# Two routings of a four-layer kernel: the operands of the rank products go from fp32 to bf16

## The chip, the cores and the metric

The kernel runs on one core of a Trainium2 chip. The metric is the device time of one execution in microseconds (us). It was timed three times; a fourth execution was recorded by the hardware profiler, and all rows of the trace come from that one.

## What is computed

The input is a batch of 4 x 1024 tokens with 128 features. Four layers follow each other, each added to its input: an attention with 16 heads (causal, rotary), a mixture of experts that sends each token to one of 8 experts, a second attention that looks at 38 fixed offsets, and a second mixture of experts that sends each token to two of 8. Cut to what matters here, the first mixture is

```
logits = x @ router_w + router_b
max_ind = jnp.argmax(softmax(logits), axis=1)
for e in range(8):
    a, g = jnp.split(x @ w1[e], 2, axis=1)
    y = silu(a) * g @ w2[e]
    out = jnp.where((max_ind == e)[:, None], y, out)
out = out * max_prob
```

and the second chooses with `top_k(logits, 2)` and adds the two experts' results with the weights of a softmax. The reference computes every expert for every token. The kernel computes only the chosen ones, and so has to sort the tokens by expert first.

## The kernel before

**The sort.** Both routings work on half a batch at a time: 4 tiles of 128 tokens, 8 halves for each routing. For a half, VectorE writes for each token and expert a 1 where the expert was chosen and a 0 elsewhere: 128 partitions (tokens) by 4 tiles by 8 experts, 32 columns. This is `r.oh`. TensorE then makes the *rank products* (`rk` in the first routing, lines 246 to 254; `rank` in the second, lines 1244 to 1253). One matmul with a strict upper triangle as weights (`tri`, 128 x 128) counts, for each token, the tokens of its tile ahead of it that chose the same expert. Three matmuls with weights of ones (`one`) add to each tile the counts of the tiles before it, and four more with the ones sum the half into 8 columns. These are 8 matmuls, each with its own load of 128 x 128 weights. VectorE adds the running `base` of each expert, picks the chosen expert's position (`rpos` at lines 299 to 309, `pos` at lines 1327 to 1337), and GpSimd scatters the token's row to that position in memory with an indirect DMA (`send0`, `send`).

**The stages.** The program has four stages with a barrier between them, and each engine walks through one written-out list of work items in each stage; each engine executes its own part of it in order.

- Attention 0 (0 to 860 us of the trace). 32 units of two heads. TensorE makes scores twice: once for the row maxima (line 561, taken by VectorE at lines 775 and 778), once for the probabilities (line 572, exponentiated by ScalarE at line 666), then the product with V (line 589). SyncE copies the rotated Q and K for four units at a time (line 495). The halves of the first three batches are routed beside it, at the steps of the table `ROUTES`. All products share a ring of three PSUM tiles S.
- Expert layer 0 (860 to 1100 us). It begins with the two halves of the last batch, interleaved with a small chain of 128 x 128 products for a matrix exponential (lines 998 and 1128). Only when the last half is ranked does VectorE know where each expert's rows end (`tiles0`), and only then can SyncE fetch the sorted rows.
- Attention 1 (1100 to 1411 us). 32 tiles of 128 tokens, with the second routing for five of its halves beside it (table `STEPS1`). TensorE makes scores at line 1540, VectorE takes them at line 1701, probabilities are transposed (line 1557) and multiplied with V (line 1566).
- Expert layer 1 (1411 to 1667 us). It begins with the other three halves of the second routing. Beside them TensorE makes the dense products `ab` (lines 1944 and 1945). When the eighth half is ranked, the sorted rows are fetched and the experts run.

**The choices' path in the second routing.** `top` (VectorE) writes `r.o0` and `r.o1`, the first and the second choice, and their sum `r.oh` (tile `ohs`, line 1326); `rank` (TensorE) waits for it; `pos` (VectorE) waits for `rank` and is queued ahead of `q3` of the next half on VectorE, whose result `n2` TensorE transposes (`nT`) before it makes the next logits (`lg1`).

**What a wait is.** `dve.then(ins)` makes VectorE wait for its own instruction `ins` before it goes on, since a read behind a write on one engine is not ordered otherwise.

I number the rank products by time: r1 to r8 for the first routing (at 367, 473, 565, 671, 764, 841, 881 and 890 us), q1 to q8 for the second (at 1245, 1288, 1333, 1374, 1402, 1453, 1469 and 1485 us).

Of the kernel before, what the change touches and what calls it, by code (L numbers as in the profile page):

```python
# [6 lines left out]
F32 = mybir.dt.float32  # L7
F32R = mybir.dt.float32r
BF16 = mybir.dt.bfloat16
U32 = mybir.dt.uint32  # L10
ALU = mybir.AluOpType
# [77 lines left out]
class Program:  # L89
# [41 lines left out]
    def sb(self, st, name, shape, dt=F32):  # L131
        return st.enter_context(self.nc.sbuf_tensor(name, shape, dt))
# [55 lines left out]
class Route0:  # L188
    loads = ("rw", "iota", "rb", "tri", "one", "base", "first", "idn")

    def __init__(self, p, st):
        def sb(name, shape, dt=F32):
            return p.sb(st, name, shape, dt)

        self.xs = p.nc.dram_tensor("xs", (8 * CAP + 128, RW0), F32, kind="Internal").ap()
        self.small = {n: sb(n + "0", [128, w]) for n, w in
                      (("rw", 8), ("iota", 8), ("rb", 8), ("tri", 128), ("one", 128), ("base", 8), ("first", 8), ("idn", NT))}
        self.lg, self.m8, self.d8, self.ex, self.oh, self.pa = (sb(n, [128, 4, 8]) for n in ("lg0", "m80", "d80", "ex0", "oh0", "pa0"))
        self.i8, self.fi, self.sm, self.posf = sb("i80", [128, 4, 8], U32), sb("fi0", [128, 4]), sb("sm0", [128, 4]), sb("posf0", [128, 4])
        self.posu, self.share = [sb(f"posu0{q}", [128, 4], U32) for q in range(3)], sb("share", [128, 32])  # L200
        self.xr, self.xT = [], []
        self.n, self.slot = {}, {}
# [32 lines left out]
def route0_tensor(p, r, pe, te, w):  # L235
    s, S, m, q = w.slot, p.S, r.small, room0(w)
    if w.kind == "rT":
        pe.wait_ge(p.sem("v_xr"), w.n)
        turn_over(te, p, S[s], r.xr[q][:, :, 0:128], 4).then_inc(p.made("rT").h, 1)
    elif w.kind == "rl":  # L240
        pe.wait_ge(p.sem("d_r0"), 16 * len(r.loads))
        pe.wait_ge(p.done("rT"), w.n)
        for i in range(4):
            ins = te.matmul(S[s][:, 8 * i:8 * i + 8], r.xT[q][:, 128 * i:128 * i + 128], m["rw"][:], start=True, stop=True)
        ins.then_inc(p.made("rl").h, 1)
    elif w.kind == "rk":
        pe.wait_ge(p.sem("v_hot"), w.n)
        oh = r.oh[:].rearrange("p n e -> p (n e)")
        te.matmul(S[s][:, 0:32], m["tri"][:], oh, start=True, stop=False)
        for d in range(1, 4):  # L250
            te.matmul(S[s][:, 8 * d:32], m["one"][:], oh[:, 0:32 - 8 * d], start=False, stop=(d == 3))
        for i in range(4):
            ins = te.matmul(S[s][:, 64:72], m["one"][:], oh[:, 8 * i:8 * i + 8], start=(i == 0), stop=(i == 3))
        ins.then_inc(p.made("rk").h, 1)


# [13 lines left out]
def route0_vector(p, r, dve, ve, w):  # L270
    S, s, m, q = p.S, w.slot, r.small, room0(w)
    n = 8 * w.at[0] + 4 * w.at[1]
    if w.kind == "rn":
        dve.wait_ge(p.sem("v_mean"), r.n[w.at])
        dve.wait_ge(p.sem("g_rstd"), r.n[w.at])
        dve.wait_ge(p.sem("d_r0"), 16 * len(r.loads))
        if not q:
            dve.wait_ge(p.sem("v_spin"), min(8 * B, 4 * (2 * w.at[0] + w.at[1] + 4)))
            if w.n > 1:
                dve.wait_ge(p.sem("d_sc0"), 64 * (w.n - 1))  # L280
        ve.tensor_copy(r.xr[q][:, :, 128:RW0], m["idn"][:, n:n + 4, None].broadcast_to([128, 4, RW0 - 128]))
        ln_apply(p, ve, r.xr[q][:, :, 0:128], p.x[:, n:n + 4, :], range(4)).then_inc(p.sem("v_xr").h, 1)
    elif w.kind == "rl":
        dve.wait_ge(p.made("rl"), w.n)
        ve.tensor_tensor(r.lg[:], S[s][:, 0:32].rearrange("p (n e) -> p n e", e=8),
                         m["rb"][:, None, :].broadcast_to([128, 4, 8]), ALU.add).then_inc(p.done("rl").h, 1)
        dve.wait_ge(p.done("rl"), w.n)
        for i in range(4):
            ins = ve.max(r.m8[:, i, :], r.lg[:, i, :])
        dve.then(ins)  # L290
        ve.tensor_tensor(r.d8[:], r.lg[:], r.m8[:, :, 0:1].broadcast_to([128, 4, 8]), ALU.subtract).then_inc(p.sem("v_negmax").h, 1)
        for i in range(4):
            ins = ve.max_index(r.i8[:, i, :], r.m8[:, i, :], r.lg[:, i, :])
        dve.then(ins)
    elif w.kind == "rhot":
        dve.then(ve.tensor_copy(r.fi[:], r.i8[:, :, 0]))
        ve.tensor_tensor(r.oh[:], m["iota"][:, None, :].broadcast_to([128, 4, 8]), r.fi[:, :, None].broadcast_to([128, 4, 8]),
                         ALU.is_equal).then_inc(p.sem("v_hot").h, 1)
    elif w.kind == "rpos":
        s = r.slot["rk", w.at[0], w.at[1]]  # L300
        dve.wait_ge(p.made("rk"), w.n)
        dve.then(ve.tensor_tensor(r.pa[:], S[s][:, 0:32].rearrange("p (n e) -> p n e", e=8), m["base"][:, None, :].broadcast_to([128, 4, 8]), ALU.add))
        ve.tensor_tensor(m["base"][:], m["base"][:], S[s][:, 64:72], ALU.add).then_inc(p.done("rk").h, 1)
        dve.then(ve.tensor_tensor(r.pa[:], r.pa[:], r.oh[:], ALU.mult))
        dve.then(ve.tensor_reduce(r.posf[:], r.pa[:], AX.X, ALU.add))
        ve.tensor_copy(r.posu[q][:], r.posf[:]).then_inc(p.sem("v_pos0").h, 1)
        dve.wait_ge(p.sem("a_ex"), w.n)
        dve.then(ve.tensor_reduce(r.sm[:], r.ex[:], AX.X, ALU.add))
        dve.then(ve.reciprocal(r.share[:, n:n + 4], r.sm[:]))
# [191 lines left out]
def attn0_tensor(p, k, pe, te):  # L501
    S, A, W = p.S, p.A, k.W
    for w in k.items:
# [3 lines left out]
        if w.kind in ("rT", "rl", "rk"):  # L507
            route0_tensor(p, k.route, pe, te, w)
# [687 lines left out]
RW, G, NC1, NQ1 = 144, 4, 8, 3  # L1196


class Route1:
    loads = ("mw", "mb", "base", "first", "idt", "cols")  # L1200

    def __init__(self, p, st, first):
        def sb(name, shape, dt=F32):
            return p.sb(st, name, shape, dt)

        def two(name, shape, dt=F32):
            return [sb(f"{name}{i}", shape, dt) for i in range(2)]

        self.xq = p.nc.dram_tensor("xq", (8 * CAP + 128, RW), F32, kind="Internal").ap()
        self.small = {n: sb(n + "1", [128, w]) for n, w in (("mw", 8), ("mb", 8), ("base", 8), ("first", 8), ("cols", 3))}  # L1210
        self.small["idt"] = sb("idt", [128, 32, 2])
        self.small.update({n: first.small[n] for n in ("iota", "tri", "one")})
        self.n1, self.nT = two("n1", [128, G, 128]), sb("nT", [128, NC1, 128 * G])
        self.n2 = [two(f"n2{q}", [128, G, RW]) for q in range(NQ1)]
        self.stats, self.mv, self.rs = sb("stats1", [128, G, 6]), sb("mv1", [128, G, 2]), sb("rs1", [128, G])
        self.lg, self.m8 = sb("lg1", [128, G, 8]), sb("m81", [128, G, 8])
        self.i8, self.fi = sb("i81", [128, G, 8], U32), sb("fi1", [128, G, 2])
        self.dd = sb("dd", [128, NT])
        self.o0, self.o1, self.oh = (sb(n, [128, G, 8]) for n in ("o0", "o1", "ohs"))
        self.pa, self.m0, self.m1 = (sb(n, [128, G, 8]) for n in ("pa", "m0", "m1"))  # L1220
        self.posf, self.posu = sb("posf", [128, 2, G]), [sb(f"posu{q}", [128, 2, G], U32) for q in range(NQ1)]
        self.bank, self.placed = {}, set()
# [10 lines left out]
def route1_tensor(p, r, pe, te, w):  # L1233
    m, c = r.small, w.at[0]
    if w.kind == "nT":
        pe.wait_ge(p.sem("v_n2"), c + 1)
        turn_over(te, p, r.bank["nT", c], r.n2[c % NQ1][0][:, :, 0:128], G).then_inc(p.made("nT").h, 1)
    elif w.kind == "lg1":
        bank = r.bank["lg1", c]
        pe.wait_ge(p.done("nT"), c + 1)  # L1240
        for i in range(G):
            ins = te.matmul(bank[:, 8 * i:8 * i + 8], r.nT[:, c, 128 * i:128 * i + 128], m["mw"][:], start=True, stop=True)
        ins.then_inc(p.made("lg1").h, 1)
    elif w.kind == "rank":
        bank = r.bank["rank", c]
        pe.wait_ge(p.sem("v_oh"), c + 1)
        oh = r.oh[:].rearrange("p n e -> p (n e)")
        te.matmul(bank[:, 0:8 * G], m["tri"][:], oh, start=True, stop=False)
        for d in range(1, G):
            te.matmul(bank[:, 8 * d:8 * G], m["one"][:], oh[:, 0:8 * (G - d)], start=False, stop=(d == G - 1))  # L1250
        for i in range(G):
            ins = te.matmul(bank[:, 64:72], m["one"][:], oh[:, 8 * i:8 * i + 8], start=(i == 0), stop=(i == G - 1))
        ins.then_inc(p.made("rank").h, 1)


# [1073 lines left out]
```

## Time and profile before

| | us |
|---|---|
| median of three timed executions | 1683.62 |
| lowest and highest of them | 1682.8 and 1690.06 |
| the profiled execution, its own time | 1668.86 |
| span of the trace, first to last instruction | 1667.1 |

The profiled execution is 14.8 us shorter than the median, so a sum in its microseconds is carried over as a difference, not as a time. Its busiest engine is TensorE (82% of the span), then VectorE (69%). The granted TensorE clock is 0.874 of full speed on average; it is always at one of two levels, 2.4 GHz (1.0) or 1.2 GHz (0.5), and the mean says how the time is shared between them.

In the rows, PE is TensorE's matmuls, PEld its weight loads, DVE VectorE, ACT ScalarE, POOL GpSimd and SPq the queue in which SyncE issues transfers. L253 is line 253 of the kernel.

### The profile page before, as it was taken

To read this page: it belongs to the slowest core of one execution; us is meant where nothing else is said; L and a number is where in the kernel's file an instruction comes from. 1 tells how busy PE (TensorE), PEld (TensorE's weight loads), DVE (VectorE), ACT (ScalarE), POOL (GpSimd) and SP (SyncE) were. 2 spreads that over 40 slices of the span, in tenths; PEclk is the share of its full clock that TensorE was granted. 3 is DMA by queue.
4 is the path that set the end of the run, shared out by engine and by line. 5 is a ranking of instruction groups with operands and counts; after the bars stand their busy time and mean duration, and the time that the engine had idled before them with its cause. 6 is when DMAs were issued, how large, how long until landed. Compare 5 with 4: busy or idle time off the path is not lost.

```text
span 1667.1 us, 37536 instructions
## 1 busy us (share of the span) xinstructions
PE 1368.6 (82%) x13404; PEld 903.3 (54%) x13404; DVE 1153.7 (69%) x3796; ACT 723.6 (43%) x1523; POOL 697.4 (42%) x1004
## 2 busy tenths in 40 slices
PE   4479889998998889989967999498898997886771
PEld 2244444454454544545446666377777776665660
DVE  4568697887979878888834544369999977144445
ACT  1135455555555545555630334155544431115553
POOL 3013232232423323342221223478878885264554
PEclk9679999999999999999975999778978776558995
DMA  4654717455373735737224011121111111212324
GB/s 101 93 95 75 116 25 113 76 89 88 46 125 53 118 56 71 125 45 124 32 98 154 24 31 40 31 71 50 41 41 47 49 49 37 77 54 72 83 79 159
DMA packets 73724, 123.13 MB, mean 74 GB/s; under 512 B 17505, under 2 KB 45928, under 8 KB 72645
## 3 DMA queue, kind: packets, MB, share of 16 engines
q1 hardware_dynamic: 64820, 106.67, 33.9%
q0 software_dynamic: 7616, 13.59, 2.5%
q8 instruction: 109, 1.79, 0.5%
q10 hardware_dynamic: 1104, 0.48, 0.1%
q14 instruction: 75, 0.61, 0.1%
HBM read 30.34 MB, written 17.60 MB: 29 GB/s over the span
## 4 chain that ended last, share of the span: by engine, by line
PE 47%; DVE 23%; SPq 11%; issue 7%; DMA 4%; ACT 4%; POOL 2%; ACTq 0%; POOLq 0%; DVEq 0%
SPq L495 9%; DVE first L775 5%; PE A L589 4%; PE S L1029 4%; PE S L572 3%; PE S L1540 3%; DVE S L778 3%; PE S L561 3%; PE A L1973 3%; PE S L1966 2%; PE A L1551 2%; DVE tA L754 2%; PE S L553 2%; PE A L1041 2%; DVE tB L755 2%
## 5 line engine op out<-in xcount | busy, mean ns | idle before, releaser
L666 ACT ACTIVATE P<-S 128x512 f32<-128x512 f32 (+3 forms) x768 | 332.2, 490 | 290.5 <-PE S L572 285.0
L561 PE MATMUL S<-Kp,Qp 120*128 120x512 f32 (+3 forms) x768 | 254.6, 401 | 43.7 <-issue 15.6
L849 POOL TENSOR_SCALAR_AFFINE_SELECT P<-P 128x256 f32<-128x256 f32 (+1 forms) x256 | 117.4, 462 | 401.5 <-ACT P L666 400.5
L572 PE MATMUL S<-Qp,Kp 121*128 121x512 f32 (+3 forms) x768 | 252.8, 393 | 32.6 <-DVE tB L755 9.2
L778 DVE CUSTOM_DVE_ANT_0 S<-S,later 128x512 f32<-128x512 f32 (+3 forms) x512 | 239.4, 514 | 50.8 <-PE S L561 43.6
L561 PEld LDWEIGHTS S<-Kp,Qp 120*128 120x128 f32 x768 | 134.5, 197 | 178.7 <-issue 80.5
L775 DVE TENSOR_REDUCE first<-S 128x1 f32<-128x512 f32 x256 | 164.5, 684 | 52.4 <-PE S L561 52.3
L572 PEld LDWEIGHTS S<-Qp,Kp 121*128 121x128 f32 x768 | 140.1, 193 | 108.9 <-issue 24.9
L589 PE MATMUL A<-P,V 128*9 128x512 f32 (+3 forms) x1536 | 176.6, 508 | 4.6 <-POOL P L849 4.2
L2104 POOL DMA_INDIRECT yq<-yq,id x71 | 69.5, 978 | 66.1 <-DVE yq L2068 35.1
L1773 POOL TENSOR_TENSOR prod<-qf,kT 128x128 f32<-128x128 f32 x160 | 73.1, 490 | 38.8 <-ACT qf L1608 20.1
L1188 POOL DMA_INDIRECT ys<-yo,id x39 | 38.2, 980 | 107.9 <-DVE yo L1168 104.0
L1540 PE MATMUL S<-kT,Qm 32*32 32x64 f32 x4096 | 64.9, 235 | 22.4 <-issue 11.9
L1352 POOL DMA_INDIRECT xq<-n,posu x64 | 68.7, 1073 | 30.1 <-DVE posu L1336 15.7
L1029 PE MATMUL S<-w,xgT 128*128 x156 | 76.8, 616 | 3.8 <-issue 2.4
L1159 DVE SCALAR_TENSOR_TENSOR uu<-th,S 128x512 f32<-128x512 f32 x39 | 26.9, 689 | 68.5 <-ACT th L1061 58.1
L778 DVE DVE_READ_ACCUMULATOR2_ANT mx<- 128x1 f32 x512 | 72.2, 141 | 0.0
L1540 PEld LDWEIGHTS S<-kT,Qm 32*32 32x32 f32 x4096 | 49.6, 110 | 39.0 <-issue 21.4
L1656 ACT ACTIVATE pt<-S 128x1024 f32<-128x1024 f32 x32 | 32.7, 1023 | 64.7 <-PE S L1557 63.5
L1973 PE MATMUL A<-er,hq 128*128 x284 | 51.2, 304 | 8.2 <-issue 3.7
L1966 PE MATMUL S<-xqT,wq 128*128 128x128 f32 x284 | 48.6, 296 | 10.7 <-ACT xqT L2002 9.9
L754 DVE TENSOR_TENSOR tA<-S,cos 128x512 f32<-128x512 f32 x60 | 41.2, 686 | 21.7 <-PE S L553 12.0
(333 smaller groups left out, 2793.5 us busy)
## 6 DMA issues: line engine op xcount, KB each, us to landing
Qp<-rcq SPq DMA_DIRECT2D x64, 256.0 KB
Kp<-rck SPq DMA_DIRECT2D x64, 256.0 KB
Qp<-rcq SPq DMA_DIRECT2D x64, 128.0 KB
Kp<-rck SPq DMA_DIRECT2D x64, 128.0 KB
xq<-xq SPq DMA_DIRECT2D x71, 72.0 KB
yb<-yq SPq DMA_DIRECT2D x8, 528.0 KB, 4.4
Qp<-cq SPq DMA_DIRECT2D x64, 64.0 KB
Kp<-ck SPq DMA_DIRECT2D x64, 64.0 KB
```

The lines of the kernel that those rows point to most:

```text
L495: ye.dma_start(rows, src).then_inc(p.sem(f"d_q{u % 4}").h, 16)
L561: te.matmul(S[s][:, 512 * h:512 * h + n], Q[0:120, h, 128 * qt:128 * qt + 128], K[0:120, h, 512 * part:512 * part + n], start=True, stop=T ...
L572: te.matmul(S[s][:, 512 * h + c:512 * h + 512], K[0:121, h, 128 * kb:128 * kb + 128], Q[0:121, h, 512 * qh + c:512 * qh + 512], start=True ...
L589: ins = te.matmul(A[oa][o:o + 9, c:512], k.V[u // 8 % 2][:, kb, 2 * (u % 8) + h, :], k.P[(e.n - 1) % NP0][:, h, c:512], start=kb < 2, stop ...
L666: se.activation(k.P[(w.n - 1) % NP0][:, h, c:512], S[s][:, 512 * h + c:512 * h + 512], ACT.Exp, scale=SCALE0).then_inc(p.done("st").h, 1)
L775: ve.tensor_reduce(k.first[:, h, qt - 4:qt - 3], S[s][:, 512 * h:512 * h + 512], AX.X, ALU.max).then_inc(p.done("mx").h, 1)
L778: ins = ve.tensor_tensor_reduce(out=of, in0=of, in1=k.later[:, 512 - n:512], scale=1.0, scalar=-3e38, op0=ALU.add, op1=ALU.max, accum_out= ...
L849: ge.affine_select(P[:, :, start:c + 128], P[:, :, start:c + 128], [[0, 2], [1, wide]], ALU.is_ge, 0.0, base=start - c, channel_multiplier ...
L1029: ins = te.matmul(S[s][:, c:c + 512], k.xgT[t % NH][:], k.w1[:, bass.ds(expert[t] * 1024 + c, 512)], start=True, stop=True)
L1540: ins = te.matmul(C[32 * q:32 * q + 32, 64 * h:64 * h + 64], k.Qm[c % 2][rows, j, 128 * i + 32 * q:128 * i + 32 * q + 32], k.kT[c % 2][row ...
L1966: ins = te.matmul(S[s][:, c], k.w[t % 4][:, c], k.xT[t % 4][:], start=True, stop=True)
L1973: ins = te.matmul(A[s][:, 0:129], k.h[t % 4][:, 128 * j:128 * j + 128], k.er[:, bass.ds(expert * 258 + 129 * j, 129)], start=(j == 0), sto ...
```

## The change

The choices `r.oh`, the triangle and the ones become bf16 tiles where a matmul reads them. All values are 0, 1 or 2 at most, which bf16 holds exactly; the sums in PSUM stay fp32.

- The triangle and the ones are still loaded in fp32, and VectorE copies each once into a bf16 tile (`tri16`, `one16`) at the first `rhot`.
- In the first routing VectorE still writes `r.oh` in fp32, because `rpos` multiplies with it; it now waits for it and copies it into a bf16 tile `hot0`. The signal `v_hot`, for which TensorE waits, moves to that copy.
- In the second routing the sum `ohs` is written as bf16 directly. It is read by the matmuls alone, so no instruction is added there.

No work item moves on any engine. VectorE gains 10 instructions (8 copies of 128 x 32, two of 128 x 128); the other engines keep theirs.

```
-        te.matmul(S[s][:, 0:32], m["tri"][:], oh, start=True, stop=False)
+        te.matmul(S[s][:, 0:32], r.tri[:], r.hot[:], start=True, stop=False)
         for d in range(1, 4):
-            te.matmul(S[s][:, 8 * d:32], m["one"][:], oh[:, 0:32 - 8 * d], start=False, stop=(d == 3))
+            te.matmul(S[s][:, 8 * d:32], r.one[:], r.hot[:, 0:32 - 8 * d], start=False, stop=(d == 3))
         for i in range(4):
-            ins = te.matmul(S[s][:, 64:72], m["one"][:], oh[:, 8 * i:8 * i + 8], start=(i == 0), stop=(i == 3))
+            ins = te.matmul(S[s][:, 64:72], r.one[:], r.hot[:, 8 * i:8 * i + 8], start=(i == 0), stop=(i == 3))
         ins.then_inc(p.made("rk").h, 1)
...
     elif w.kind == "rhot":
         dve.then(ve.tensor_copy(r.fi[:], r.i8[:, :, 0]))
-        ve.tensor_tensor(r.oh[:], m["iota"][:, None, :].broadcast_to([128, 4, 8]), r.fi[:, :, None].broadcast_to([128, 4, 8]),
-                         ALU.is_equal).then_inc(p.sem("v_hot").h, 1)
+        dve.then(ve.tensor_tensor(r.oh[:], m["iota"][:, None, :].broadcast_to([128, 4, 8]), r.fi[:, :, None].broadcast_to([128, 4, 8]), ALU.is_equal))
+        if w.n == 1:
+            ve.tensor_copy(r.tri[:], m["tri"][:])
+            ve.tensor_copy(r.one[:], m["one"][:])
+        ve.tensor_copy(r.hot[:], r.oh[:].rearrange("p n e -> p (n e)")).then_inc(p.sem("v_hot").h, 1)
...
-        self.o0, self.o1, self.oh = (sb(n, [128, G, 8]) for n in ("o0", "o1", "ohs"))
+        self.o0, self.o1, self.oh = (sb(n, [128, G, 8], dt) for n, dt in (("o0", F32), ("o1", F32), ("ohs", BF16)))
...
-        te.matmul(bank[:, 0:8 * G], m["tri"][:], oh, start=True, stop=False)
+        te.matmul(bank[:, 0:8 * G], r.tri[:], oh, start=True, stop=False)
         for d in range(1, G):
-            te.matmul(bank[:, 8 * d:8 * G], m["one"][:], oh[:, 0:8 * (G - d)], start=False, stop=(d == G - 1))
+            te.matmul(bank[:, 8 * d:8 * G], r.one[:], oh[:, 0:8 * (G - d)], start=False, stop=(d == G - 1))
         for i in range(G):
-            ins = te.matmul(bank[:, 64:72], m["one"][:], oh[:, 8 * i:8 * i + 8], start=(i == 0), stop=(i == G - 1))
+            ins = te.matmul(bank[:, 64:72], r.one[:], oh[:, 8 * i:8 * i + 8], start=(i == 0), stop=(i == G - 1))
```

## Rows read from the trace of the kernel before

**Rows 1.** Windows; busy PE, PEld, DVE, ACT, POOL; granted clock, DMA share, GB/s

```profile
1180.00:1415.00 235.00, 204.55 (x5104) 171.79 (x5093) 209.99 (x565) 93.39 (x139) 184.06 (x251) 0.77 0.16 45
1415.00:1508.00 93.00, 72.01 (x262) 56.55 (x262) 28.11 (x164) 13.65 (x21) 35.36 (x39) 0.54 0.20 67
```

**Rows 2.** Line 1330's answer: what it waited for, us in total, times

```profile
  PE A L1252: 18.8, 3
```

**Rows 3.** Chain that ended last, at r1: start us, us, what

```profile
367.61 0.14 PE S L249 x2
367.75 0.65 PE S L251 x6
368.40 0.89 PE S L253 x8
```

**Rows 4.** The same chain at r8

```profile
890.72 0.27 PE S L249 x2
890.98 1.24 PE S L251 x6
892.22 1.71 PE S L253 x8
```

**Rows 5.** The same chain at q7

```profile
1469.08 0.56 PE A L1248 x2
1469.64 1.24 PE A L1250 x6
1470.88 1.72 PE A L1252 x8
```

**Rows 6.** The same chain behind q1, products with V

```profile
1247.32 0.67 PE A L1566 x50
```

**Rows 7.** The same chain between r1 and r3, beside r2

```profile
470.96 1.97 SPq L495
```

**Rows 8.** Timeline, VectorE in attention 0: start, us, line; idle before it, releaser

```profile
369.33 0.19 DVE L302 TENSOR_TENSOR pa<-S,base 128x32 f32<-128x32 f32 x1 [0.47 <-PE S L253]
371.89 1.29 DVE L775 TENSOR_REDUCE first<-S 128x1 f32<-128x512 f32 x2 [0.66 <-PE S L561]
...
570.49 1.29 DVE L775 TENSOR_REDUCE first<-S 128x1 f32<-128x512 f32 x2 [0.94 <-PE S L561]
...
767.87 0.69 DVE L775 TENSOR_REDUCE first<-S 128x1 f32<-128x512 f32 x1 [0.34 <-PE S L561]
...
843.37 0.19 DVE L302 TENSOR_TENSOR pa<-S,base 128x32 f32<-128x32 f32 x1 [1.98 <-PE S L253]
```

**Rows 9.** Timeline, VectorE at the start of expert layer 0

```profile
880.15 0.16 DVE L296 CAST fi<-i 128x4 f32<-128x4 uint32 x1
880.34 0.19 DVE L297 TENSOR_TENSOR oh<-iota,fi 128x32 f32<-128x32 f32 x1
...
883.70 0.19 DVE L302 TENSOR_TENSOR pa<-S,base 128x32 f32<-128x32 f32 x1 [0.73 <-PE S L253]
...
890.75 0.56 DVE L1128 TENSOR_TENSOR F<-S,G 128x384 f32<-128x384 f32 x1 [1.50 <-PE S L998]
...
893.97 0.19 DVE L302 TENSOR_TENSOR pa<-S,base 128x32 f32<-128x32 f32 x1 [2.26 <-PE S L253]
```

**Rows 10.** Timeline, VectorE: a copy of 128 x 128

```profile
1418.37 0.22 DVE L2038 COPY Rg<-R 128x128 f32<-128x128 f32 x1
```

**Rows 11.** Timeline, VectorE behind q2, q3 and q4

```profile
1306.98 1.23 DVE L1701 TENSOR_TENSOR sc<-S,near 128x1024 f32<-128x1024 f32 x1 [0.43 <-PE S L1540]
...
1341.10 1.22 DVE L1701 TENSOR_TENSOR sc<-S,near 128x1024 f32<-128x1024 f32 x1 [2.96 <-PE S L1540]
...
1386.19 0.24 DVE L1704 TENSOR_TENSOR sc<-A,far 128x80 f32<-128x80 f32 x1 [1.02 <-PE A L1551]
```

**Rows 12.** Timeline, GpSimd's indirect DMAs ahead of and behind q8

```profile
1483.58 0.96 POOL L1352 DMA_INDIRECT xq<-n,posu  x1 [0.31 <-issue]
...
1490.37 1.16 POOL L1352 DMA_INDIRECT xq<-n,posu  x1 [5.83 <-DVE posu L1336]
```

More of the change, by code:

```diff
@@ L198, in __init__ @@
         self.lg, self.m8, self.d8, self.ex, self.oh, self.pa = (sb(n, [128, 4, 8]) for n in ("lg0", "m80", "d80", "ex0", "oh0", "pa0"))
+        self.hot = sb("hot0", [128, 32], BF16)
+        self.tri, self.one = sb("tri16", [128, 128], BF16), sb("one16", [128, 128], BF16)
         self.i8, self.fi, self.sm, self.posf = sb("i80", [128, 4, 8], U32), sb("fi0", [128, 4]), sb("sm0", [128, 4]), sb("posf0", [128, 4])
@@ L247, in route0_tensor @@
         pe.wait_ge(p.sem("v_hot"), w.n)
-        oh = r.oh[:].rearrange("p n e -> p (n e)")
-        te.matmul(S[s][:, 0:32], m["tri"][:], oh, start=True, stop=False)
+        te.matmul(S[s][:, 0:32], r.tri[:], r.hot[:], start=True, stop=False)
         for d in range(1, 4):
-            te.matmul(S[s][:, 8 * d:32], m["one"][:], oh[:, 0:32 - 8 * d], start=False, stop=(d == 3))
+            te.matmul(S[s][:, 8 * d:32], r.one[:], r.hot[:, 0:32 - 8 * d], start=False, stop=(d == 3))
         for i in range(4):
-            ins = te.matmul(S[s][:, 64:72], m["one"][:], oh[:, 8 * i:8 * i + 8], start=(i == 0), stop=(i == 3))
+            ins = te.matmul(S[s][:, 64:72], r.one[:], r.hot[:, 8 * i:8 * i + 8], start=(i == 0), stop=(i == 3))
         ins.then_inc(p.made("rk").h, 1)
@@ L1211, in __init__ @@
         self.small["idt"] = sb("idt", [128, 32, 2])
-        self.small.update({n: first.small[n] for n in ("iota", "tri", "one")})
+        self.small["iota"], self.tri, self.one = first.small["iota"], first.tri, first.one
         self.n1, self.nT = two("n1", [128, G, 128]), sb("nT", [128, NC1, 128 * G])
```

## The prediction

> **What bounds the kernel now.** I read the page first. TensorE is busy 82% of the span and VectorE 69%, so a saving of TensorE time can count, but neither number says where. The windows by stage say more [rows 1]: in the middle of attention 1 (235 us) VectorE is busy 210.0 us and TensorE 204.6 us, two engines about equally close to the bound; at the start of expert layer 1 (93 us) TensorE is busy 72.0 us at a granted clock of 0.54, almost all at the lower level, and VectorE only 28.1 us. The time of a rank product is therefore worth something different at each of its 16 places. So I read the chain that ended last at each place, then the waits of VectorE behind it in the timeline.
>
> At full clock a rank product is 16 records, two for each of its 8 matmuls, and takes 0.14 + 0.65 + 0.89 = 1.68 us of the chain, 0.105 us a record [rows 3]. At the lower level it is 0.27 + 1.24 + 1.71 = 3.22 us, 0.201 us a record [rows 4]. The columns (32, 24, 16 or 8) make no difference that one can see, so it is the weights that are paid for. r1 to r7, q1, q2, q3 and q5 ran at the full level, r8, q4, q6, q7 and q8 at the lower one.
>
> **Price of a bf16 matmul.** The trace has no bf16 matmul. The upper bound is one record as it stands, 0.105 us (0.201 at the lower level): half the records, none of them faster. The lower bound is the cheapest record in the trace, line 1566 with 32 columns of weights: 0.67 us for 50, 0.013 us each [rows 6]. Those load a quarter of the columns; four of them would be 0.054 us. Between ends eight times apart I go by that row, scaled to the columns, and take half a record: 0.0525 us, or 0.10 us at the lower level. A product then costs 8 x 0.0525 = 0.42 us instead of 1.68, or 0.80 us instead of 3.22: it saves 1.26 us at full clock and 2.42 us at the lower one. By the bounds it saves 0.84 to 1.57 us, or 1.61 to 3.11 us.
>
> The Trainium skill, page "TensorE: Matmul & The Clock Gate", section "LDWEIGHTS (loading the stationary operand)", speaks against the half record: a load takes as many ns as its columns divided by 1.2, and no type is named there, which for 128 columns is 107 ns. That is close to the trace's record at full clock, and by it the saving would be near my lower bound. The page "FP8 and Floating Point Precision" of the Trainium skill, section "TensorE Precision Notes", has true fp32 as 4 passes through the array, which by itself gives a quarter. No run so far tells them apart.
>
> **Attention 0.** VectorE gains a wait for its own comparison and a small copy in each `rhot`. A conversion and the comparison behind it, with the same kind of wait between them, start 0.19 us apart [rows 9], so I take 0.2 us a place. The two copies of 128 x 128 come once, ahead of r1: 0.22 us for such a copy [rows 10], less where one overlaps the next, so 0.35 us for both. Behind the `rhot`, TensorE is still busy with queued scores for 2 to 3 us, so `v_hot` coming later holds up no matmul; what it costs is VectorE's own time, where VectorE leads to the next scores.
> - r1: VectorE waits 0.47 us for the product and 0.66 us for scores right behind it [rows 8]. These 1.13 us are what it can get back, less 0.2 and 0.35: 0.6 us.
> - r3: 0.47 (as at r1) and 0.94 us [rows 8], more than the 1.26 us saved; less 0.2: 1.1 us.
> - r5: 0.47 and 0.34 us [rows 8], less 0.2: 0.6 us.
> - r2 and r4: nothing. Around r2 the chain is SyncE's issue of one transfer after the other [rows 7], and around r4 too; TensorE ends by waiting for the last of them.
> - r6: VectorE waits 1.98 us for it [rows 8] and ScalarE waits for the scores behind it: all of 1.3 us.
>
> Sum 3.6 us. By the bounds of the price 2.4 us, or 4 x 1.57 = 6.3 us without the copies.
>
> **Expert layer 0.** The copy is hidden: after r8's comparison VectorE waits 1.50 us for TensorE anyway [rows 9]. At r7 VectorE waits 0.73 us for the product, because it has work for line 1131 until then; more it can't get back. At r8 it waits 2.26 us of the 2.42 [rows 9]; the product of line 998 queued behind r8 starts when VectorE's line 1131 lets it, so of these I take 2.0. The ends of the experts' rows, the pads, the fetches of sorted rows and the matrix exponential all follow. Sum 2.7 us; bounds 0.7 + 1.6 = 2.3 and 0.73 + 2.26 = 3.0 us.
>
> **Attention 1.** Nothing is added on VectorE. A shorter product counts only if VectorE next waits for TensorE. Behind q1 it has no such wait before q2, and behind q5 TensorE waits for VectorE: 0. Behind q2 the first wait is 0.43 us, behind q3 2.96 us (so all 1.26), behind q4 1.02 us [rows 11]. Sum 2.7 us. The bounds are 0, if TensorE's lead runs into the next slot of PSUM each time, and 9.4 us, if every product counts whole at the cheapest price (4 x 1.57 + 3.11).
>
> **Expert layer 1.** Here the products stand bare in the chain: q7 is 0.56 + 1.24 + 1.72 us, of which 0.29 is the first record's latency and stays [rows 5]. VectorE waits 18.8 us in three times for q6, q7, q8 and the dense products ahead of them [rows 2], and everything of the next half is queued on VectorE behind `pos`. So 3 x 2.42 = 7.3 us. GpSimd could take the place: its indirect DMAs of the halves before run one behind the other until 1484.5 us, and it then waits 5.83 us for q8's positions [rows 12]. That stream moves ahead with q6 alone (2.42 us), q8's positions with all three (7.3): 4.9 of the 5.83 us are used, and 0.9 stays. It is not late yet. Bounds 3 x 1.61 = 4.8 us, and 5.83 + 3.11 = 8.9 us, where GpSimd becomes the later.
>
> **Sum.** 3.6 + 2.7 + 2.7 + 7.3 = 16.3 us. From the profiled execution's 1668.86 us that gives 1652.6; from the median of 1683.62, which is 14.8 us higher for the same program, 1667.3, rounded to 1667. The bounds are 2.4 + 2.3 + 0 + 4.8 = 9.5 us and 6.3 + 3.0 + 9.4 + 8.9 = 27.6 us, so 1656.0 to 1674.1.
>
> **The rivals.**
> - *A bf16 load is no cheaper than a record.* All products save the lower bound: 9.5 us, 1674. For it: the record's time doesn't depend on the moving columns [rows 3]. This is where the rule on LDWEIGHTS of the Trainium skill, page "TensorE: Matmul & The Clock Gate", would end. Chance 0.12.
> - *VectorE takes it all in the attentions.* Nothing is gained there and the copies are paid in full, 6 x 0.2 + 0.35 = 1.6 us: 2.7 + 7.3 - 1.6 = 8.4 us, 1675. For it: its 210.0 busy us of 235 [rows 1], and that in attention 0 the chain passes through it as much as through TensorE. Against: the waits of rows 8. Chance 0.12.
> - *More comes back.* TensorE is really the bound in attention 1 as well, as the chain there says, which lies on it behind every product: 5 us more there and the cheaper load elsewhere, some 25 us, 1659. Chance 0.12.
> - *Slower: the granted clock.* Attention 1 runs at 0.77 [rows 1], so 46% of it at the lower level. Where TensorE has less to do it has been granted the lower level: 0.54 at the start of expert layer 1, with 72.0 busy us of 93. If shorter products tip more of attention 1 to it, its 204.6 busy us stretch with 0.77 over the new clock. A clock of 0.713 eats the whole 16.3 us; from 0.69 on the kernel is slower by over 0.5%; at 0.68 it is 27 - 16 = 11 us, 1694. Against: q1 to q5 are under 5% of that stage's TensorE work. Chance 0.06.
>
> **Chances and range.** 0.58 for the forecast, whose own range is 1661 to 1673, and the rest as above. A measurement of this kernel tells about 0.5%, 8.4 us, from no change. The forecast and the rival with more end below 1675.2 but for small parts; of the first two rivals, which lie within a microsecond of that line, I count half. That is 0.54 + 0.12 + 0.12 = 0.78 for faster, 0.15 for within 0.5%, 0.07 for slower. The range takes in the bounds of the price and, above, a few of the 7 us by which the three timed executions differ: 1656 to 1679.
>
> **What the next profile would show.** One record for each matmul in place of two (line 1252's group on the ring A: 12, not 24), 0.05 us apart at full clock. VectorE's three waits at the line after `rank` fall from 18.8 to about 11.5 us, and GpSimd's wait ahead of q8's sends to about 1 us. From the start of expert layer 1 to its first expert the time falls by 7 us. Attention 1 shortens by less than its products do, and VectorE's busy time stays. The forecast is wrong if records are 0.1 us apart (price), if the last half's positions come 7 us earlier but its transfers don't (GpSimd or SyncE), or if the clock of attention 1 moves by more than 0.03 either way, which alone is worth 8 us.

## The result, and the profile after

| | median, us | runs, us | ratio to before, 95% interval |
|---|---|---|---|
| before, beside it | 1683.21 | 1678.27 to 1690.06 | |
| the change | 1665.26 | 1651.54 to 1671.35 | 0.9900, 0.9854 to 0.9945 |
| the change in a later job | 1666.07 | 1656.06 to 1672.9 | 0.9918, 0.9882 to 0.9953 |

The change is 14 to 17 us faster. The two profiled executions don't show it: 1668.86 us before, 1668.63 us after. So I read the trace by stage and over all profiles of the study, never by the difference of two spans.

The windows of [rows 1], in the profile of the change:

```profile
1180.00:1415.00 235.00, 200.63 (x4818) 164.81 (x4816) 203.06 (x553) 89.36 (x133) 173.13 (x240) 0.70 0.14 40
1415.00:1508.00 93.00, 68.11 (x242) 51.79 (x243) 28.07 (x164) 14.29 (x22) 35.58 (x39) 0.50 0.19 67
```

TensorE is busy 4 us less in each. The granted clock is lower in both, 0.70 for 0.77 and 0.50 for 0.54. In the first, attention 1, the 4 us hide two larger terms, which are taken apart below.

The chain that ended last, at q7, beside [rows 5]:

```profile
1469.74 0.14 PE A L1252
1469.88 0.07 PE A L1254 x3
1469.95 0.12 PE A L1256 x4
1470.07 0.02 issue
1470.09 0.20 DVE pa L1334
```

One record a matmul in place of two, and the product is 0.14 + 0.07 + 0.12 = 0.33 us at the lower level, where it was 3.52 us. The matmuls stand 0.02 to 0.03 us apart, though a load by itself lasts 0.1 us: they overlap. At full clock (r6) it is the same:

```profile
835.71 0.12 PE S L250
835.83 0.07 PE S L252 x3
835.89 0.10 PE S L254 x4
```

What VectorE waited for at line 1334 (before line 1330, [rows 2]), and then the timeline at q8, GpSimd and SyncE's queue included:

```profile
  remote: 7.4, 1
  PE A L1256: 5.8, 2
```

The three waits are 13.2 us together, where the prediction had about 11.5. At q8:

```profile
1482.86 0.25 PE L1256 MATMUL A<-ohs,one 128*128 128x8 bf16 x4
1483.28 0.95 POOL L1356 DMA_INDIRECT xq<-n,posu  x1 [0.30 <-issue]
1484.54 0.96 POOL L1356 DMA_INDIRECT xq<-n,posu  x1 [0.30 <-issue]
1486.62 0.19 DVE L1334 TENSOR_TENSOR pa<-A,base 128x32 f32<-128x32 f32 x1 [7.37 <-remote]
1488.01 1.16 POOL L1356 DMA_INDIRECT xq<-n,posu  x1 [2.52 <-DVE posu L1340]
1488.77 12.15 SPq L1908 DMA_DIRECT2D xq<-pads  x8
...
1502.93 0.36 SPq L1918 DMA_DIRECT2D xq<-xq  x1
```

Here is something that I had not foreseen. The product's last matmul ends at 1482.86 + 0.25 = 1483.11 us. VectorE waits for that alone and starts 3.5 us later; the trace calls the releaser "remote", which means that it has none. GpSimd's wait, 5.83 us in [rows 12], is 2.52 us. SyncE's eight pads (the rows that fill up each expert's last tile) then take 12.15 us to issue and the first rows are fetched 2.0 us behind the last. At q6 a send (an indirect DMA that GpSimd issues) runs across the product's end too, and VectorE starts 0.03 us behind the product:

```profile
1456.79 0.25 PE L1256 MATMUL A<-ohs,one 128*128 128x8 bf16 x4
1456.99 0.96 POOL L1356 DMA_INDIRECT xq<-n,posu  x1 [0.30 <-issue]
1457.07 0.19 DVE L1334 TENSOR_TENSOR pa<-A,base 128x32 f32<-128x32 f32 x1 [4.30 <-PE A L1256]
```

### The profile page after: what moved, and what is told of

It is laid out like the page before. It is cut to its first block, busy times and chain, and to the rows that moved or that the text cites. A ratio compares the mean times of both kernels' runs of the same rounds, so it can differ in the third digit from the quotient of the medians.

```text
span 1666.7 us, 37290 instructions
## 1 busy us (share of the span) xinstructions
PE 1358.0 (81%) x13276; PEld 888.0 (53%) x13276; DVE 1156.7 (69%) x3806; ACT 723.5 (43%) x1523; POOL 693.7 (42%) x1004
## 4 chain that ended last, share of the span: by engine, by line
PE 43%; DVE 25%; SPq 9%; issue 8%; POOL 5%; DMA 5%; ACT 4%; another core or an unknown queue 1%; ACTq 0%; POOLq 0%; DVEq 0%
SPq L499 8%; DVE first L779 5%; PE S L1033 4%; PE A L593 4%; DVE S L782 3%; PE S L576 3%; PE S L565 3%; PE S L1544 3%; PE A L1977 2%; PE S L1970 2%; PE A L1555 2%; PE A L1045 2%; DVE tA L758 2%; PE S L179 2%; PE S L557 2%
## 5 line engine op out<-in xcount | busy, mean ns | idle before, releaser
L1544 PE MATMUL S<-kT,Qm 32*32 32x64 f32 x4096 | 66.0, 244 | 18.4 <-issue 7.2
```

The costliest lines, as they stand in the source:

```text
L1544: ins = te.matmul(C[32 * q:32 * q + 32, 64 * h:64 * h + 64], k.Qm[c % 2][rows, j, 128 * i + 32 * q:128 * i + 32 * q + 32], k.kT[c % 2][row ...
```

## The experiments

Twelve runs in three jobs, each job with its own runs of the kernel before. Two of them repeat a kernel: the change, and the version without copies.

**1. One routing at a time.** In the first, only the first routing is bf16, with the copies. In the second only the second, without `hot`; the two copies of 128 x 128 stay. A part of the edit of the first, against the change (triangle and ones go back to fp32 as well):

```diff
-        self.o0, self.o1, self.oh = (sb(n, [128, G, 8], dt) for n, dt in (("o0", F32), ("o1", F32), ("ohs", BF16)))
+        self.o0, self.o1, self.oh = (sb(n, [128, G, 8], dt) for n, dt in (("o0", F32), ("o1", F32), ("ohs", F32)))
```

> Only the first routing's rank products (r1 to r8) are bf16, with the copies of the change; the second routing's are fp32 as before. My sum gives it 3.6 us in attention 0 and 2.7 us in expert layer 0: ratio to the kernel before about 0.996. If VectorE takes the gain in attention 0, as the two profiles hint (4.5 of the first 7.4 us by which the changed kernel is ahead at the end of attention 0 are there before r1), only expert layer 0 counts: 1.5 to 2.5 us, ratio 0.999.

> Only the second routing's rank products (q1 to q8) are bf16; the first routing's are fp32 as before, without its small copy (the two copies of the triangle and the ones remain). My sum gives 2.7 us in attention 1 and 7.3 us in expert layer 1: ratio about 0.994. If a bf16 matmul costs 0.03 us, as the changed kernel's profile shows, the three products of expert layer 1 give 8 to 9 us. If the granted clock of attention 1 falls with it (0.70 in the changed kernel's profile, 0.77 before), nothing may be left: ratio 0.998 to 1.0.

Measured: 0.9958 (0.993 to 0.9986) and 0.9968 (0.9936 to 0.9999) of 1680.02 us, 7.0 and 5.4 us. The first routing gives about what I forecast (6.3 us), the second about half (10.0), each with an interval of some 5 us either way. The alternative for the first, a ratio of 0.999, lies outside. The second's profile shows where more is lost at q8:

```profile
1488.60 14.65 SPq L1909 DMA_DIRECT2D xq<-pads  x8
1499.33 1.08 ACT L1993 ACTIVATE ab<-S 128x512 f32<-128x512 f32 x2 [15.24 <-remote]
1505.26 0.36 SPq L1919 DMA_DIRECT2D xq<-xq  x1
```

VectorE's positions are 3 us earlier than in the kernel before, but the pads take 14.65 us to issue, and ScalarE too waits for something that the trace doesn't have. The kernel before, same rows:

```profile
1491.13 10.93 SPq L1904 DMA_DIRECT2D xq<-pads  x8
1504.07 1.49 SPq L1914 DMA_DIRECT2D xq<-xq  x2
```

**2. bf16 without a copy.** Triangle and ones come from memory as bf16, and the comparison writes its 0 and 1 as bf16 itself; the positions are still fp32. The change once more and a repeat of this version follow. The edit against the change, in part:

```diff
-        self.hot = sb("hot0", [128, 32], BF16)
+        self.oh = sb("oh0", [128, 4, 8], BF16)
...
-        dve.then(ve.tensor_tensor(r.oh[:], m["iota"][:, None, :].broadcast_to([128, 4, 8]), r.fi[:, :, None].broadcast_to([128, 4, 8]), ALU.is_equal))
-        if w.n == 1:
-            ve.tensor_copy(r.tri[:], m["tri"][:])
-            ve.tensor_copy(r.one[:], m["one"][:])
-        ve.tensor_copy(r.hot[:], r.oh[:].rearrange("p n e -> p (n e)")).then_inc(p.sem("v_hot").h, 1)
+        ve.tensor_tensor(r.oh[:], m["iota"][:, None, :].broadcast_to([128, 4, 8]), r.fi[:, :, None].broadcast_to([128, 4, 8]),
+                         ALU.is_equal).then_inc(p.sem("v_hot").h, 1)
...
-        "tri": (k[:, None] < k[None, :]).astype(np.float32),
+        "tri": (k[:, None] < k[None, :]).astype(mybir.dt.np(BF16)),
```

> The change without its copies: the triangle and the ones arrive as bf16 from memory, and the first routing writes its choices as bf16 directly and multiplies with them in that type. VectorE loses 10 instructions and 8 waits for itself, 2 us of its own time. If VectorE bounds attention 0, it is 1 to 2 us faster than the change (ratio to before about 0.989); if the copies are hidden, the same as the change.

> The change once more, unaltered, against the kernel before. Both theories have it at 1665 to 1668 us, a ratio of 0.990 to 0.992. What it settles is whether the version with the 0/1 operands written as bf16 at their source (1657.66 us, ratio 0.987, in an earlier job) is really faster than the change: the seven VectorE copies that it drops in the first routing's ramp and row are worth 8 x 0.2 us plus two of 0.22 us at most, so theory 1 (the copies cost what they last) has the two 2 us apart or less, and a gap of 5 us or more here again would mean that something other than the copies' own time is saved. The wait of VectorE's first instruction behind the eighth rank product of the second routing ends again some 3 us after the product does if that stall belongs to the kernel, and at once if it was chance.

> The version with no copy at all, once more, beside the two above: 1653 to 1659 us, ratio 0.985 to 0.988 in each theory. The add behind the eighth product of the second routing starts 2 to 3.5 us late again, since GpSimd's sends run at that moment.

Measured: 1657.66 us, 0.9870 (0.9839 to 0.9902), and in another job 1652.56 us, 0.9846 (0.9796 to 0.9895). The change again is 1666.07 us, 0.9918. The gap of 5 us or more that theory 1 excluded is there again, though in different jobs. Beside the change itself ran a version without copies with 60 idle writes added (part 5): 0.9862 for 0.9918, 9 us, give or take 10. Over all, two measurements with the copies have a mean ratio of 0.9909 and the four without the small ones 0.9861 (the three here and one of part 3): 8 us, give or take 6. So the copies cost more than the 1.6 us that I had given them.

**3. Which copy.** The first has bf16 choices at the source but still copies triangle and ones once; the second is the kernel before, fp32 throughout, with all of the change's copies added, read by nobody. A part of the second's edit against the change:

```diff
-        te.matmul(S[s][:, 0:32], r.tri[:], r.hot[:], start=True, stop=False)
+        oh = r.oh[:].rearrange("p n e -> p (n e)")
+        te.matmul(S[s][:, 0:32], m["tri"][:], oh, start=True, stop=False)
```

> The change with the 0/1 choices of the first routing written as bf16 by the comparison itself, so that the eight copies hot and their waits are gone; triangle and ones are still copied once. Stage times of the profiles so far, attention 0 from the second addition to x to its end: 559 to 562 us in three profiles with copies, 554 to 556 in three without, 562 to 571 with fp32. Theory K (the eight copies, with the add of their own wait and the 0.62 us that one lasts beside GpSimd, cost those 5 us): this one lies with the version without any copy, 1654 to 1659 us, ratio 0.985 to 0.988. Theory L (the two 128x128 copies in the first row cost it, one of them 0.57 us at 358): it lies with the change, 1664 to 1667 us. Theory M (5 us are where chance put those six profiles): all three are alike within 2 us in this job.

> The kernel before, all products in fp32, with only the change's copies and their waits added (their results are read by nobody). Theory K: 4 to 6 us slower than before, ratio 1.0025 to 1.0035. Theory L: the same 4 to 6 us. Theory M: 8 x 0.23 us and the row's 0.4 us at most, under 2 us, ratio 1.000 to 1.001. If copies cost 5 us with fp32 too, their price is VectorE's and not that of the earlier start of anything.

Measured: 1656.23 us, 0.9866 (0.9814 to 0.9918), where the versions without copies lie; and 1683.93 us, 1.0041 (1.0001 to 1.0081), so 7 us slower by the ratio, with an interval from 0.2 to 14 us. The times point to theory K, that it is the eight small copies and their waits, but don't show it: the first kernel alone, set against the change, is 7 us better with an interval of 10 either way, and the second has all ten copies. A part of the cost can be seen. VectorE's copy beside a mask of GpSimd's, in the profile of the change at r3:

```profile
556.07 0.62 POOL L853 TENSOR_SCALAR_AFFINE_SELECT P<-P 128x512 f32<-128x512 f32 x1 [0.47 <-ACT P L670]
556.10 0.62 DVE L302 CAST hot<-oh 128x32 bf16<-128x32 f32 x1
...
664.83 0.18 DVE L302 CAST hot<-oh 128x32 bf16<-128x32 f32 x1
```

It ends when GpSimd's instruction does, 0.62 us instead of 0.18. That happens to one or two of eight, to the copy of the triangle as well (0.57 us); with the starts 0.23 us apart and 0.62 us for the two of the first row the sum is 8 x 0.23 + 2 x 0.44 + 0.62 = 3.3 us at most. The rest I can't place.

**4. Doubled, and six times.** All fp32 rank products of the kernel before issued twice; those of the second routing alone; and in the version without copies the bf16 products of the first routing six times. The edit of the second routing, in part:

```diff
-        te.matmul(bank[:, 0:8 * G], m["tri"][:], oh, start=True, stop=False)
+        for _ in range(2):
+            te.matmul(bank[:, 0:8 * G], m["tri"][:], oh, start=True, stop=False)
```

> The kernel before with every fp32 rank product issued twice (the second overwrites the first with the same sums). TensorE gets 1.68 us more at full clock or 3.22 us more at the lower level at 16 places. If TensorE's time at these places counts as in my sum, the loss is 1.2 to 1.3 times the forecast gain, 20 us, ratio 1.012. If VectorE hides them in the attentions, only the start of the two expert layers counts: 3 x 3.22 + 1.7 + 3.2 = 14.6 us, ratio 1.009. If a longer busy TensorE is granted more of the full clock in attention 1, it is less than that.

> The kernel before with its eight fp32 rank products of the second routing issued twice; the first routing is as before. Both routings doubled cost 45 us, where the products' own time, all of it on the path, is 8 x 1.68 us for the first routing and 5 x 1.68 + 3 x 3.22 us for the second, 31 us in all. If each routing is amplified alike, this one costs 22 to 28 us (1702 to 1708 us); if the extra in both was the first routing's (20 us in attention 0 and 9 us ahead of expert layer 0 in that profile), it costs 10 to 18 us (1690 to 1698 us).

> The version with no copy, with each bf16 product of the first routing issued six times, 48 multiplications in place of 8. Eight more of them take 0.25 to 0.29 us in a row by the records of the change, so five more products add 1.25 to 1.45 us to each of eight places, about what the fp32 form had more than the bf16 form (1.68 less 0.33 us). If TensorE's time in the row is all that counts, this takes back what the first routing won without copies: 8 x 1.35 = 11 us, 1664 to 1668 us. If extra TensorE time in attention 0 is amplified, as doubling fp32 there seemed to say (45 us for both routings less 20 for the second leaves 25 us for 13.4 us of products), it is 18 to 22 us, 1674 to 1678 us.

Measured: 1.0273 (1.0224 to 1.0322), 1.0112 (1.0057 to 1.0167) and 0.9863 (0.9811 to 0.9915). The first is 46 us (38 to 54), more than twice the 20 that I expected. I had scaled the forecast gain, which is capped where VectorE's wait ends, while added time has no such cap: all the products are 33.1 us, at the levels of the clock that they had before. The levels moved too: r7, at full clock before, ran at the lower one in both of its copies. Doubling the second routing costs 19 us by the ratio, what its products are worth with all of them on the path (5 x 1.68 + 3 x 3.22 = 18.1 us). The first routing takes the other 0.016, 27 us, give or take 12, for 7 x 1.68 + 3.22 = 15.0 us of products; whether that is more than they are worth isn't shown. Six bf16 products in a row, at r1:

```profile
364.36 0.19 PE L252 MATMUL S<-oh,tri 128*128 128x32 bf16 x1
364.40 0.22 PE L254 MATMUL S<-oh,one 128*128 128x24 bf16 x3
364.47 0.24 PE L256 MATMUL S<-oh,one 128*128 128x8 bf16 x4
364.57 0.18 PE L252 MATMUL S<-oh,tri 128*128 128x32 bf16 x1
364.60 0.22 PE L254 MATMUL S<-oh,one 128*128 128x24 bf16 x3
364.67 0.24 PE L256 MATMUL S<-oh,one 128*128 128x8 bf16 x4
364.77 0.18 PE L252 MATMUL S<-oh,tri 128*128 128x32 bf16 x1
```

A product takes 0.20 us, 0.025 a matmul. Five more at each of eight places are 8.0 us of TensorE, not the 11 that I expected; the ratio has moved by 0.0017 against the same version with single products in the same job, 3 us, with an interval that takes in 8 and 0 but not the 18 to 22 us of an amplified cost. In its one profile attention 0 is 6.5 us longer than in the five others without the small copies (563.3 for a mean of 556.8), and the products added there are 6 x 1.0 us: what is added is about what is paid.

**5. The late start at q8.** In the version without copies: first 60 short VectorE writes more, hidden in a 7 us wait, which shift its instruction stream; second, four of GpSimd's sends held back until the last positions are there.

```diff
+    for j in range(12):
+        for t in k.yo:
+            ve.memset(t[:, 8 * j:8 * j + 1], 0.0)
```

```diff
-        pool.wait_ge(p.sem("v_pos"), c + 1)
+        pool.wait_ge(p.sem("v_pos"), NC1 if (c, h) == (NC1 - 2, 1) else c + 1)
```

> The version without copies, with 60 short VectorE writes of one column more at the start of expert layer 1, where VectorE waits 7 us for a load and has nothing else to do. It moves every later VectorE instruction 60 places down its instruction stream and costs nothing on the path (60 x 0.07 us = 4 us inside a 7 us wait). Theory S (the late start behind the eighth rank product is the stream being fetched): the late start of 2.0 to 3.5 us moves away from that place or changes to under 0.5 us. Theory G (something of GpSimd's sends, which run at that moment): it stays at 2 us or more. Theory C (chance): it is gone, and e5 and e7 show it or not without pattern. Time as the version without copies, 1655 to 1661 us, in each theory.

> The version without copies, with the last four sends of the seventh group (second half of its rows) held back on GpSimd until the positions of the eighth group are there. GpSimd is then idle when the eighth rank product ends. Theory G: VectorE's add behind that product starts within 0.3 us of the product's end. Theory S: still 2 to 3 us late. In both the sends end later: GpSimd has 12 sends of 1.26 us behind the eighth positions instead of 8, so expert layer 1's first expert starts 5 us later less what the earlier positions give back (2 to 3 us in theory G): about 1660 us.

The stream shifted:

```profile
1467.41 0.25 PE L1254 MATMUL A<-ohs,one 128*128 128x8 bf16 x4
1467.85 0.96 POOL L1354 DMA_INDIRECT xq<-n,posu  x1 [0.30 <-issue]
1469.12 0.96 POOL L1354 DMA_INDIRECT xq<-n,posu  x1 [0.30 <-issue]
1470.41 0.19 DVE L1332 TENSOR_TENSOR pa<-A,base 128x32 f32<-128x32 f32 x1 [6.60 <-remote]
```

The sends held back:

```profile
1468.90 0.25 PE L1254 MATMUL A<-ohs,one 128*128 128x8 bf16 x4
1469.19 0.19 DVE L1332 TENSOR_TENSOR pa<-A,base 128x32 f32<-128x32 f32 x1 [3.88 <-PE A L1254]
...
1470.57 1.16 POOL L1354 DMA_INDIRECT xq<-n,posu  x1 [4.07 <-DVE posu L1338]
```

Shifted, VectorE is 2.75 us late as before. Held back, it starts 0.04 us after the product, and the wait has its releaser again. In the eight profiles with bf16 in the second routing and the sends running it is 2.0 to 3.5 us late each time; in the five with fp32 never, since there the product ends when the sends are through. That speaks for theory G, that the late start needs GpSimd's row of sends, and against theory S; but the held-back case has one profile, and the sends alone don't do it: in the same eight profiles a send is under way or begins within 0.25 us at the end of q6's product, and VectorE starts there within 0.04 us of it. What holds VectorE up, the runs don't say. Holding back wins nothing here, since the sends end later (first fetch 17.7 us behind `endi`; one execution, 1654.05 us); the shifted version is 1653.61 us, 0.9862 (0.9817 to 0.9907), a third measurement without copies.

## The stages, over all profiles

Worked out from the timelines, one profile a kernel: attention 0 from VectorE's second to its eighth addition to x, attention 1 from its first to its eighth, the start of expert layer 0 up to the first fetch of sorted rows, that of expert layer 1 from q6's logits (line 1312 before) to the copy `endi`, and from there to the first fetch. The number of profiles stands in brackets. Doubled products are left out, and the six-fold and held-back kernels where they touch the stage.

| stage, us | fp32 there | bf16 there | gain | forecast |
|---|---|---|---|---|
| attention 0, no copies `hot` | 561.9, 570.7, 565.5 | 555.4, 556.4, 554.1, 558.1, 560.0 | 9.2 | |
| attention 0, with copies | 566.2 | 558.9, 560.9, 561.7 | | 3.6 |
| start of expert layer 0 | 46.1 to 48.3 (4) | 42.8 to 44.4 (8) | 3.4 | 2.7 |
| attention 1 | 225.9, 238.2, 241.5 | 225.7 to 234.5 (9) | open | 2.7 |
| expert layer 1, q6 to `endi` | 43.1 to 45.1 (3) | 36.7 to 39.3 (8) | 6.7 | 7.3 |
| `endi` to first fetch | 14.1 (5) | 14.2 to 18.4 (8), mean 16.2 | -2.1 | 0 |

## Why the prediction was right, point by point

Forecast 1667 us, measured 1665.3, inside the likeliest case's own range. That the sum came within 2 us is luck: errors of opposite sign met, and one stage is open by more than its term. The mechanism held in attention 0 and expert layer 0, and in expert layer 1 up to the last positions.

- **The price.** Half a record, 0.0525 us and 0.10 us at the lower level, was too dear: it is 0.025 us in a row at full clock, and a product alone is 0.29 to 0.33 us at either level. From `pos` of q6 to that of q7 is 16.18 us before and 13.02 after, 3.16 us saved where the step said 2.42. The row with 32 columns was the nearest, and scaling it by the columns was the mistake: 0.013 us became 0.054, and it is 0.025. The rule on LDWEIGHTS of the Trainium skill, page "TensorE: Matmul & The Clock Gate", section "LDWEIGHTS (loading the stationary operand)", fits the record of one load and not the spacing: 107 ns for 128 columns is near the records of r1 to r8 (95 to 99 ns for most), but loads follow each other in 0.025 us. The rival built on it falls.
- **Attention 0: 3.6 us.** The mechanism was right, both sizes were off. Capping each product by VectorE's next wait, and putting r2 and r4 at nothing, made the gross gain too small: without the copies `hot` the stage is 9 us shorter (mean 566.0 to 556.8, though the three in fp32 alone span 9 us), and 6 x (1.68 - 0.33) = 8.1 us is all six in full. At r2 VectorE waited for the product as well, before:

```profile
475.24 0.19 DVE L302 TENSOR_TENSOR pa<-S,base 128x32 f32<-128x32 f32 x1 [0.90 <-PE S L253]
```

  It did so at r4, and in the profiles of bf16 it waits for neither, nor for r1, r3 and r5, if the products are single. The term for the copies was too small as well: with them the stage is 5.5 us shorter than in fp32 without them, 3.7 us less of a gain. Yet fp32 with copies (566.2) is no longer than fp32 without, so the profiles don't place the copies' cost in this stage. The rival in which VectorE takes the whole gain falls here.
- **Expert layer 0: 2.7 us.** Measured 3.4, a little over the bound of 3.0 that I had set from VectorE's two waits.
- **Attention 1: 2.7 us.** Open. In fp32 this stage took 226 to 242 us without a change in it, which swamps the term. I had written that a clock more than 0.03 away would make the forecast wrong. It did move, 0.77 to 0.70 and 0.69 in the two profiles of the change, and the stage took 233.3 and 234.5 us for 225.9: by my own sign the forecast failed in this stage, and the total came out all the same.

  The step behind the slower rival, TensorE's work stretching as the clock falls, is seen in part. TensorE was busy 201.3 us before and 203.9 and 202.8 after, but of these the rank products are 11.3 before and 1.8 after. All its other work went from 190.1 to 202.1 and 201.0 us, 11 to 12 us more, where the rival's rule of 0.77 over the new clock would have 19 to 22. In the other profiles without doubled products that work is 189 us at 0.77, 193 to 195 at 0.73 to 0.75 and 197 to 200 at 0.72. The stage's length doesn't follow in step (226.1 us at 0.72 with bf16 in the second routing alone), and what is cause here and what effect the profiles don't say.

  Another thing goes with the long stage: all four profiles of kernels with the eight copies in attention 0, 400 us earlier, took 233.3 to 241.5 us there, whatever the type of the products, and the eight others without doubled products 225.7 to 228.7. Against it stand the two doubled kernels, which have no copies: 250.4 and 238.6 us, and less what their products take more (29.0 and 29.6 us for 11.3) still 232.7 and 220.3, 12 us apart.

  The fp32 kernel with copies, over the stretch from first to eighth addition:

```profile
1185.20:1426.70 241.50, 212.65 (x4912) 178.67 (x4911) 205.24 (x556) 90.74 (x135) 177.35 (x244) 0.72 0.14 40
```

  and the bf16 kernel without, second measurement:

```profile
1170.40:1398.40 228.00, 196.31 (x4863) 163.19 (x4862) 204.69 (x556) 91.62 (x135) 176.39 (x244) 0.73 0.15 43
```

  The clock is nearly the same and VectorE as busy; TensorE is busy 16.3 us more, 11.1 of it the fp32 products. I have no mechanism. The difference is of the size by which the times differ (8 us), so this may be where the copies' cost lies, but that is a correlation over twelve profiles.
- **Expert layer 1: 7.3 us.** The positions came early as forecast (6.7 us, with a cheaper product, less the late start at q8). Then 2.1 us were given back. I had named GpSimd as next in line, with 0.9 us to spare. It was SyncE's row of eight pads: in the kernel before it already set the first fetch, 10.93 us and 2.0 us more, and I had no term for it. It takes 10.9 to 11.0 us in five profiles with fp32 and 11.1 to 14.65 us in the nine with bf16; why it is longer there is open. Net 4.6 us.

Stage gains of 5.5 + 3.4 + 4.6 = 13.5 us stand against 14 to 17 us measured, but attention 1 is left out of them. With the 8 us by which it was longer in the change's profiles 5.5 us would be left, so the stages don't add up to the times: with one profile of the kernel before, attention 1 can't be set against itself. The best version is the one without copies: 1652.6 to 1657.7 us, 1.3 to 1.5% under the kernel before and some 8 us under the change.

## What to carry to other kernels

A 0/1 operand should be born in the type in which TensorE wants it, written so by the comparison or loaded so, since the copies, 0.2 us each for the most part, seem to cost some 8 us (2 to 14), about a third of what the version without them gains. Where a product stands bare between a wait and its reader, count it whole, and then follow the stage to the queue that issues its transfers: the next in line was a row of eight small issues that had been the last link all along. And where one stage varies by 10 us from run to run, compare stages over several profiles before a difference of two spans is explained.

## What the runs showed of the hardware

- A bf16 matmul with 128 columns of weights and 8 to 32 moving ones takes 0.025 us in a row (six products behind each other at r1, 0.20 us each); in fp32 it is 0.21 us at full clock and 0.40 at the lower level, 8 and 16 times as much. The bf16 row was the same at both levels: 0.07 us of the chain for three and 0.10 to 0.12 for four.
- An engine can start 2 to 3.5 us after the TensorE product that it waits for: VectorE at q8 in 8 of 8 profiles in which GpSimd was issuing a row of indirect DMAs, not in the one in which it was held back. The row isn't enough for it: at q6, with such a DMA under way or about to start, VectorE was never late. In three of the eight ScalarE too waited 15.2 us for no releaser near line 1990, where two waits of 5.2 to 7.5 us each are usual.
- A VectorE copy of 128 x 32 from fp32 to bf16 lasts 0.18 us, and 0.53 to 0.62 us when a GpSimd mask runs beside it; it ends when that does.
